# A two-layer graph network of 64 stages: one engine meeting at a stage's end for two, earlier parameter reads, row statistics inside two MLPs

## The reference

```python
xn = LN(x)
for l in range(2):                       # _L0_gnn: edge attention, 8 heads of 32
    q, k, v = h @ Wq, h @ Wk, h @ Wv     # h = xn at first
    a = exp(e - max_dst e);  e = sum(q[dst] * k[src]) / sqrt(32)
    h = LN(segment_sum(v[src] * a / z[dst]) @ Wo + h) * g + b
x = x + relu(h @ w1 + b1) @ w2 + b2  +  hyperbolic_mixer(xn)
y = LN(x)                                # _L0_ffn: an MLP on the top half of the rows by y @ wr
x = x + y + where(selected, (gelu(y @ w1 + b1) @ w2 + b2) * (y @ wr), 0)
xn = LN(x)
conv = segment_sum((xn @ W)[src] * norm) # _L1_gnn
y = xn
for l in range(4):                       # _L1_mix: linear-attention transformer
    q, k, v = softmaxes of LN(y) @ Wq, LN(y) @ Wk; LN(y) @ Wv
    y = y + (q @ (k.T @ v)) @ Wo + bo
    y = y + gelu(LN(y) @ W1 + b1) @ W2 + b2
x = x + conv + y
xn = LN(x)                               # _L1_ffn: graph attention (4 heads of 4) over 65,536 edges
scores = LN16(gat(xn @ W_gat)) meaned over heads;  top 2 of 4 experts, softmax weights
x = x + sum_e gate_e * (gelu(xn @ W1[e] + b1[e]) @ W2[e] + b2[e])
```

## Time and profile before

| | |
|---|---|
| time, median of 3 runs | 7004.79 us (7004.34 to 7008.51) |
| the profiled execution's own time | 6997.66 us |
| its span | 6995.9 us |
| PE, PEld busy | 5115.3, 3841.5 us (73%, 55%) |
| DVE busy | 4527.9 us (65%) |
| ACT busy | 2380.0 us (34%) |
| POOL busy | 4021.1 us (57%) |
| both edge-attention stages | 829.9 to 1984.7 and 2174.1 to 3325.4 us |
| rank MLP, its norm | 3410.4 to 3625.3, to 3645.3 us |
| token selection, routed MLP | to 3712.4, to 3915.6 us |
| norm, table pass, first transformer norm | to 3934.0, to 4007.4, to 4034.6 us |
| the transformer's four layers | to 5847.5 us, MLPs 235.5, 236.1, 235.5, 249.1 |
| experts | 5895.0 us to the end |

### The profile page before, as it was taken

One profiled execution on the slowest core, in us unless ns is written; L12 is line 12 of the kernel. 1 busy time (PEld: TensorE's weight loads), 2 busy tenths in 40 slices (PEclk: granted clock), 3 DMA queues, 4 the chain that ended last, 5 costly groups with the idle time before them and its releaser, 6 DMA issues. The chain is left out here.

```text
span 6995.9 us, 102505 instructions
## 1 busy us (share of the span) xinstructions
PE 5115.3 (73%) x27238; PEld 3841.5 (55%) x27238; DVE 4527.9 (65%) x7921; ACT 2380.0 (34%) x6607; POOL 4021.1 (57%) x4040
## 2 busy tenths in 40 slices
PE   3445588888857888887667579979889896877722
PEld 1334455555535555555556457768667575666611
DVE  8468499999966999998592375474654735211166
ACT  3143155555532555555212222222222221222210
POOL 1566577777737777775017656556555561577710
PEclk9777798999978999999888889989999997888855
DMA  2000377777725777775200223324333242222101
GB/s 43 24 1 5 113 224 220 219 219 218 219 62 160 224 222 220 218 217 158 54 14 7 66 72 104 110 68 115 88 92 112 64 125 67 46 45 59 25 2 59
DMA packets 362048, 766.30 MB, mean 110 GB/s; under 512 B 133276, under 2 KB 189493, under 8 KB 360552
## 3 DMA queue, kind: packets, MB, share of 16 engines
q0 software_dynamic: 232848, 605.63, 31.9%
q1 hardware_dynamic: 128707, 154.57, 7.3%
HBM read 717.16 MB, written 42.74 MB: 109 GB/s over the span
## 5 line engine op out<-in xcount | busy, mean ns | idle before, releaser
L1802 POOL DMA_INDIRECT arena<-kv_rows,visit_src x1616 | 1641.2, 1016 | 575.1 <-issue 467.6
L2378 POOL DMA_INDIRECT arena<-piece_rows,visit_src x808 | 798.6, 988 | 554.9 <-PE ps L2440 259.3
L2063 ACT CAST ps<-cat 125x265 bf16 x1616 | 619.6, 383 | 671.7 <-issue 385.5
L1955 PE MATMUL ps<-arena,w 125*128 x4848 | 787.3, 312 | 81.1 <-DVE stage_ht L1842 64.6
L924 POOL DMA_INDIRECT sorted<-arena,cat x512 | 541.1, 1057 | 514.4 <-PEq L91 338.5
L1955 PEld LDWEIGHTS ps<-arena,w 125*128 125x128 bf16 x4848 | 515.2, 106 | 373.6 <-issue 202.1
L2809 POOL DMA_INDIRECT arena<-tab,visit_src x537 | 512.6, 955 | 185.9 <-issue 172.3
L2064 ACT COPY arena<-ps x1616 | 604.6, 374 | 0.3
L924 POOL DMA_INDIRECT by_low<-steer x400 | 389.2, 973 | 373.3 <-PEq L91 162.3
L848 PE MATMUL ps<-stage_ht,w 128*128 128x250 f32 (+1 forms) x2496 | 555.9, 379 | 18.2 <-DVE stage_ht L880 13.1
L2459 DVE TENSOR_TENSOR arena<-arena,ps 125x256 f32 x808 | 340.1, 421 | 318.0 <-PE ps L2440 242.9
(11 more groups left out here) (605 smaller groups left out, 9697.0 us busy)
## 6 DMA issues: line engine op xcount, KB each, us to landing
w<-rel SPq DMA_DIRECT2D x102, 500.0 KB
arena<-kv_rows,visit_src POOLq DMA_INDIRECT x1616, 4.5
arena<-rel SPq DMA_DIRECT2D x34, 512.0 KB
arena<-piece_rows,visit_src POOLq DMA_INDIRECT x808
kv_rows<-h SPq DMA_DIRECT2D x50, 250.0 KB
arena<-tab,visit_src POOLq DMA_INDIRECT x537
sorted<-arena,cat POOLq DMA_INDIRECT x512
w<-in_L_mix_W SPq DMA_DIRECT2D x8, 1024.0 KB
```

The source lines that it names most:

```text
L1802: nc.gpsimd.indirect_dma_start(ring[k % RG][:, j, :], None, d.kv, bass.IndirectOffsetOnAxis(g.srcv[:, v:v + 1], 0)).then_inc(got[k % RG], 16)
L1955: ins = nc.tensor.matmul(psQ[:, j * D:(j + 1) * D], ohT[b % 4][:, e:e + EP], q[:, bass.ds(at[j], D)], start=(m == 0), stop=(m == 2))
L2063: nc.scalar.copy(flat[0:P, bass.ds(clean[j], WIDE)], zeros[:, 0:WIDE]).then_inc(s["zeroed"], 1)
L2378: nc.gpsimd.indirect_dma_start(self.rows[v % (self.RG * GG)], None, self.d.pieces, bass.IndirectOffsetOnAxis(g.srcv[:, v:v + 1], 0)).then_ ...
```

## The change

Five edits.

1. `phase`: the second meeting goes. In its place the numbers cleared by a stage "rest": they are allocated again at once under another name and released after the next stage's block, so that the next stage gets other numbers and the one after it may have them. As POOL's clears now go by runs of neighbouring numbers, the built program has 97 range clears for 76.
2. `graph_attention_layer`: the marks of POOL's scatters end three tiles earlier (second layer) and five earlier (first).
3. The norms of `routed_ffn` and `graph_convolution` issue no scatters and take no statistics. The rank MLP and the routed MLP take them, DVE one for each tile after its adds. The 24 scatters go to the routed MLP (162 for 150) and to the table pass (58 for 46).
4. The eight norms of the transformer's layers have no scatters. The first layer's first norm still has its gathers. Each QKV stage has 14 scatters for 10.
5. `experts`: the five rows of small parameters are fetched on SP's queue behind expert 0's weights, in the experts' norm, to places of their own; the two `loaded` waits become one wait for that fetch, in the table stage.

```diff
--- before.py
+++ after.py
@@ -35,8 +35,8 @@
-TABLE = 46
-INQKV, SOFT, INOUT, INMLP = 10, 16, 10, 23
+TABLE = 58
+INQKV, SOFT, INOUT, INMLP = 14, 16, 10, 23
@@ -90,8 +90,15 @@
     sems = [nc.alloc_semaphore(f"{n}_{COUNT[0]}") for n in names]
     with nc.Block() as block:
         yield block, dict(zip(names, sems))
+    for rested in RESTING:
+        nc.release_semaphore(rested)
+    RESTING.clear()
+    numbers = [sem.num for sem in sems]
     nc.clear_and_free_semaphores(sems)
-    nc.all_engine_barrier()
+    RESTING.extend(nc.alloc_semaphore(f"resting_{COUNT[0]}_{n}", num=n) for n in numbers)
+
+
+RESTING = []
@@ -1650,11 +1657,11 @@
             if not first:
                 g.proj_w.wait(pool)
                 nc.gpsimd.dma_start(d.h_kept, g.h).then_inc(s["side_b"], 16)
-                scatter.send_along(pool, left, EC - left, s["down"], range(1, NT + 1))
+                scatter.send_along(pool, left, EC - left, s["down"], range(1, NT - 2))
                 scatter.all_landed(pool)
                 pool.wait_ge(s["side_b"], 16)
             if first:
-                scatter.send_along(pool, left, EC - TAIL - left, s["down"], range(1, NT + 1))
+                scatter.send_along(pool, left, EC - TAIL - left, s["down"], range(1, NT - 4))
                 scatter.all_landed(pool, EC - TAIL)
@@ -2094,8 +2101,9 @@
 def routed_ffn(nc, g, a, d, scatter):
...
-    layernorm(nc, g, x, xn, side=together(scatter.beside(12), fetching(
-        (g.mlp_w, big_weights(g, a["L0_ffn_w1"], a["L0_ffn_w2"])), (g.small_b, small_weights(g, a["L0_ffn_b1"], a["L0_ffn_b2"])))))
+    layernorm(nc, g, x, xn, side=together(fetching(
+        (g.mlp_w, big_weights(g, a["L0_ffn_w1"], a["L0_ffn_w2"])), (g.small_b, small_weights(g, a["L0_ffn_b1"], a["L0_ffn_b2"])))),
+              counted=True)
@@ -2190,7 +2198,7 @@
     mlp(nc, g, xn, 1024, ACT.Gelu_apprx_tanh, x, g.coef[:, 0:NT], ready=[g.mlp_w, g.small_b],
-        side=together(scatter.along(150, "up", range(0, 4 * (NT + 1) // 2)), fetching((g.conv_w, [(w3(g.cat[:, 0:512], 2, D), split_k(a["L1_gnn_W"], 2))]),
+        stats=x, side=together(scatter.along(162, "up", range(0, 4 * (NT + 1) // 2)), fetching((g.conv_w, [(w3(g.cat[:, 0:512], 2, D), split_k(a["L1_gnn_W"], 2))]),
                                                     (g.proj_w, mixer_proj(g, a, 0)))))
@@ -2317,7 +2325,7 @@
 def graph_convolution(nc, g, a, d, scatter):
-    layernorm(nc, g, g.x, g.h, side=together(scatter.beside(12), before_layer(g, a, 0)))
+    layernorm(nc, g, g.x, g.h, side=before_layer(g, a, 0), counted=True)
     table_pass(nc, g, d, scatter)
     return Convolution(nc, g, d, scatter)
@@ -2465,8 +2473,7 @@
-    side = conv.beside(0, places=2, behind=2 if l else 0)
-    layernorm(nc, g, y, None, side=together(side, before_layer(g, a, l)) if l else side, counted=l > 0)
+    layernorm(nc, g, y, None, side=before_layer(g, a, l) if l else conv.beside(0), counted=l > 0)
@@ -2618,8 +2625,8 @@
     for l in range(4):
         linear_attention(nc, g, a, d, l, conv)
-        layernorm(nc, g, y, None, side=together(conv.beside(0, places=2, behind=2), fetching(
-            (g.small_b, small_weights(g, a["L1_mix_b1"][l], a["L1_mix_b2"][l]) + per_row(g, a["L1_mix_ln2_g"][l], a["L1_mix_ln2_b"][l])))),
+        layernorm(nc, g, y, None, side=fetching(
+            (g.small_b, small_weights(g, a["L1_mix_b1"][l], a["L1_mix_b2"][l]) + per_row(g, a["L1_mix_ln2_g"][l], a["L1_mix_ln2_b"][l]))),
                   counted=True)
         upcoming = (g.proj_w, mixer_proj(g, a, l + 1)) if l < 3 else (
             g.conv_w, [(w3(g.cat[:, 1536:1568], 2, 16), split_k(a["L1_ffn_W_gat"], 2))])
@@ -3108,7 +3115,11 @@
                  (one.brow, a["L1_ffn_b2"][e].rearrange("(a n) -> a n", a=1))]
         return fetching((one.here, big_weights(one, a["L1_ffn_W1"][e], a["L1_ffn_W2"][e]) + small))
-    layernorm(nc, g, x, xn, side=weights_of(0))
+    par = g.view(38816, 48, P)
+    aS, aD = g.view(38864, 16, P), g.view(38880, 16, P)
+    rows = [(par[:, 16 * n:16 * n + 16], a["L1_ffn_" + b].partition_broadcast(P)) for n, b in enumerate(("b_gat", "ln_gamma", "ln_beta"))]
+    rows += [(ap, a["L1_ffn_att_" + b].rearrange("h e -> (h e)").partition_broadcast(P)) for ap, b in ((aS, "src"), (aD, "dst"))]
+    layernorm(nc, g, x, xn, side=together(weights_of(0), fetching((g.small_a, rows))))
@@ -3129,14 +3140,11 @@
     tmp = g.view(13300, NT * 16, P)
-    aS, aD = g.view(13800, 16, P), g.view(13820, 16, P)
...
-    with phase(nc, g, "loaded", "step", "table", "ad", "spare", "stored", "ad_stored", "ad_back") as (block, s):
+    with phase(nc, g, "step", "table", "ad", "spare", "stored", "ad_stored", "ad_back") as (block, s):
         @block.sync
         def _(sp):
-            sp.dma_start(aS, a["L1_ffn_att_src"].rearrange("h e -> (h e)").partition_broadcast(P)).then_inc(s["loaded"], 16)
-            sp.dma_start(aD, a["L1_ffn_att_dst"].rearrange("h e -> (h e)").partition_broadcast(P)).then_inc(s["loaded"], 16)
             sp.wait_ge(s["spare"], 1)
             sp.dma_start(d.adt[N:WINDOWS * 128, :], spare[0:WINDOWS * 128 - N, :]).then_inc(s["ad_stored"], 16)
@@ -3153,7 +3161,7 @@
             V = nc.vector
             step = Steps(dve, s["step"])
             V.memset(spare, 0.0).then_inc(s["spare"], 1)
-            dve.wait_ge(s["loaded"], 32)
+            g.small_a.wait(dve)
@@ -3194,14 +3202,9 @@
-    par, scr, cmpb, rk4, ex, lower = take(48), take(100), take(400), take(100), take(100), take(16)
+    scr, cmpb, rk4, ex, lower = take(100), take(400), take(100), take(100), take(16)
...
-    with phase(nc, g, "loaded", "lowset", "step", "var", "std", "shifted", "expd") as (block, s):
-        @block.sync
-        def _(sp):
-            for n, b in enumerate((a["L1_ffn_b_gat"], a["L1_ffn_ln_gamma"], a["L1_ffn_ln_beta"])):
-                sp.dma_start(par[:, 16 * n:16 * n + 16], b.partition_broadcast(P)).then_inc(s["loaded"], 16)
-
+    with phase(nc, g, "lowset", "step", "var", "std", "shifted", "expd") as (block, s):
         @block.gpsimd
         def _(pool):
@@ -3229,7 +3232,6 @@
             step(V.tensor_tensor(s4, s4, rz.unsqueeze(2).to_broadcast([P, NT * H, EX]), ALU.mult))
-            dve.wait_ge(s["loaded"], 48)
             step(V.tensor_tensor(S3, S3, par[:, 0:16].unsqueeze(1).to_broadcast(w16), ALU.add))
@@ -3328,7 +3330,7 @@
             graph_attention_layer(nc, g, d, a["L0_gnn_Wo"][l], a["L0_gnn_ln_g"][l], a["L0_gnn_ln_b"][l], upcoming[l],
...
         rank = RankByHigh(nc, g, d, by_low)
-        mlp(nc, g, g.h, 1024, ACT.Relu, g.x, g.unit, ready=[g.mlp_w, g.small_b], weave=rank)
+        mlp(nc, g, g.h, 1024, ACT.Relu, g.x, g.unit, ready=[g.mlp_w, g.small_b], weave=rank, stats=g.x)
...
         by_dst = Scatter(nc, d.sorted, rank.places_i, rank.packed)
         routed_ffn(nc, g, a, d, by_dst)
```

## The result

The changed kernel took 6930.65 us (median of 4 runs, 6925.52 to 6933.11), the kernel before 7006.65 beside it (4 runs, 7004.34 to 7008.67): ratio 0.9898, 95% interval 0.9885 to 0.991. The forecast was 6934, the range 6912 to 6962. The two profiled spans are 6995.9 and 6928.6, 67.3 apart, the medians 76.0, for a sum of 70.7.

What follows compares the result with a forecast made beforehand. No one bound: each of 64 stages costs what its latest engine costs at the meeting. Terms -28 -11.1 -22.7 +9.3 -18.2 = -70.7 from the median 7004.8 give 6934 us, range 6912 to 6962.

Steps and rivals of the forecast that it cites:

- Second meeting, -28: At all 64 stage ends: removing the second meeting lets engines start earlier, less in POOL-led stages; -28 us, bounds -34 and 0.
- Marks, -7.8 and -3.3: Two attention projection stages: earlier scatter marks leave SP last in the first, -7.8 us; POOL paces the second, -3.3.
- Short norms, -22.7: Transformer norms without scatters: -15.1 before three layers, -6.6 before MLPs, -2.5 in the first, 1.5 charged for uncovered loads.
- Rank MLP, +4.5: Rank MLP: 25 added statistics lengthen DVE's late pairs; +4.5 us, bounds +1 and +12, the latter by PE's clock.
- Its norm, -9.2: Norm after the rank MLP: loses statistics, their loop and 12 scatters; -9.2 us.
- the convolution's, -8.6: Norm of the convolution: DVE loses 8.27 us and 0.3 of start; -8.6 us.
- Routed MLP, +10.0: Routed MLP, 162 scatters for 150: POOL already last, without pause in the steady part; 15.2 less 5.1 idle, +10.0 us.
- table pass, +12.6: Table pass, 58 scatters for 46: POOL already last, without pause; 15.2 less 2.6 idle, +12.6 us, bounds +5 and +15.
- Small parameters, -18.2: Earlier fetch ends DVE's waits: -2.6 us in the expert table stage, -15.6 for the gate stage, kept rows late next by 1.8.
- the code fetch: Rival: at each stage start a code fetch takes the meeting's place, first term about 0; 6962 us, chance 0.08.
- POOL's giving back: Rival: POOL ends four QKV stages later by 2 each, and both moved scatter lots cost their upper bound; 6950, chance 0.15.
- The fall of the clock: Rival: PE's granted clock falls in the edge-attention stages, some 90 us show; 7024 us, chance 0.02.

Runs made afterwards that it cites:

- the run with one meeting alone: The kernel before with only the second meeting removed and the cleared numbers resting, no other edit: 6974.8 us, ratio 0.9956.
- My later expectation of 6898: Expected for the changed kernel with scatters 144 in routed MLP, 40 in table pass, 13 per out projection, 29 per transformer MLP; measured 6905.9 us, ratio 0.9858.
- the whole spread with the levelled weave: Changed kernel with ranking rewoven in the rank MLP, scatters spread wider (136 in routed MLP, 40 in table pass), marks ended earlier there: 6870.1 us, ratio 0.9806.

## Why the prediction was right

By its own steps:

- **Second meeting, -28.** Put back 27.5 by spans, alone 28.6 by medians, 21 to 24 without the three stages that vary most. The size is right within what the runs tell; that two readings fall on 28 is in part luck. I charged POOL-led stages with 0.4 of 0.5; the runs don't resolve that part, as such stages vary by more than that.
- **Marks, -7.8 and -3.3.** -7.9 and -2.6, undone +7.5 and +1.9. Both signs and the new last engine are as said. The first size hits by luck: POOL stood 5.9 to 7.8 behind SP in the three kernels with all marks, and the stage varies by 4.5 with the same code. In the second stage POOL and SP meet within 0.1 us; its size, less than 1 us off, is not told apart from noise.
- **Short norms, -22.7.** The three before layers -15.8 without their meetings (15.1), the four before MLPs -7.2 (6.6), the first -2.4 (2.5); undone 26.0 in all, for 24.2. The 1.5 charged for what is uncovered was not there, and the QKV stages hide four more scatters, as costed.
- **Rank MLP, +4.5.** +5.3, undone 5.7, and 5.0 against the run with one meeting alone. This is a size that was off: I took off 1.5 for holes in DVE's late stream, and they went from 2.9 us (two pairs) to 2.1 only, which makes the term 5.2. The bound of +12 by the clock was not needed: PE's slow groups are there in both traces (8.5 to 9.8 us after idle gaps of 2 to 4 us, 7.04 else), and DVE sets the pace meanwhile. By the Trainium skill's "TensorE: Matmul & The Clock Gate", section HAM oscillation, the term would have been nearer +10; the groups agree with it, the stage's length doesn't, since there was slack in PE.
- **Its norm, -9.2; the convolution's, -8.6.** -9.0 and -9.3. In the first the statistics alone are 7.9, 1.3 under the term, and the meeting has the rest; in the second -8.8 against the run with one meeting alone.
- **Routed MLP, +10.0; table pass, +12.6.** +10.0 and +11.0, POOL last in both. But the terms were for the scatters, and taking 12 out of each gave 11.5 and 11.4: the first is 1.5 over its term and the second 1.2 under, and the routed MLP's +10.0 is 11.5 less the 1.5 that one meeting alone took off that stage. So its hit is luck. The reading behind the first term was wrong: before, POOL did not idle 8.6 us in the first pairs, but 3.7, and 5.4 in six waits for marks later on. The step "no pause in the steady part" holds at 162, not at 150. In both stages 12 scatters closed some 5 us of idle time and lengthened POOL's end behind the last scatter by 1.0, for which the sum had nothing. My later expectation of 6898 missed by the same step.
- **Small parameters, -18.2.** -2.9 and -15.3 without three meetings, and +2.8, +18.3, -2.0 when undone. The kept rows were late next, as the price assumed: a wait of 2.58 and not 1.8.

Of the rivals, the code fetch falls with the two runs on the meeting, and by "Runtime: NRT & Kernel Launch", section Instruction fetch mechanics, of the Trainium skill a gap would have had to appear behind the release, where ACT's work still starts 0.1 behind it. The two pauses in the norm behind the rank MLP, 0.7 us longer in all without the meeting, are the one sign for it. POOL's giving back falls with the QKV stages. The fall of the clock didn't come, as the windows of both edge-attention stages show (the first for the last line of the earlier trace rows):

```profile
821.50:1972.50 1151.00, 930.39 (x4605) 627.05 (x4605) 1040.45 (x1579) 634.08 (x2074) 821.70 (x808) 0.90 0.73 211
2156.80:3307.20 1150.40, 931.61 (x4605) 628.78 (x4605) 1040.11 (x1579) 635.50 (x2075) 826.13 (x808) 0.90 0.73 211
```

The granted clock is 0.90 in both. The first is 3.5 us shorter than before, which is within what it varies by.

That the sum was near is also the work of opposite errors: the scatters in the routed MLP are 1.5 over their term and the rank MLP 0.8, the scatters in the table pass are 1.2 under, and the 1.5 charged for uncovered loads didn't come. Which engine ends each edited stage was right in every term.

## What to carry to other kernels

When all engines meet after each stage, price an edit by the distance between the last and the second last engine at that meeting, and read both from the drains; that held here for the marks and the short norms. An engine that is last in a stage costs its own pace for each instruction given to it, less what it idled (15.2 us of scatters cost 11.5), and nothing in a stage where it is done early, so small background work belongs to the stages with room: moving 24 scatters gave 23 us of stage time, and the whole spread with the levelled weave 60 us. Background work that is spread over progress marks must have its last mark earlier than the stage's end by the time of its last pieces and of the tail behind them, or fewer pieces gain next to nothing.

## What the runs showed of the hardware

POOL's drain at a meeting is long behind scatters: 10.6, 13.4 and 15.6 us behind 136, 150 and 162 in the routed MLP, 17.0 behind 58 in the table pass, 3.3 behind two in a norm and 7.4 behind two beside 2 MB of loads, 52 ns with none. It isn't all waiting for data. The drain's record begins while POOL still issues; in the changed kernel's routed MLP it begins at 3886.8, and this is the last scatter:

```profile
3897.27 0.96 POOL L931 DMA_INDIRECT sorted<-arena,cat  x1 [0.31 <-issue]
```

It ends at 3898.2, and POOL arrives at 3902.4. So of 15.6 us 11.4 are scatters and 4.2 come behind the last one. That tail is 3.2 behind 150 in the run with the scatters moved to the transformer's MLPs, 2.4 behind 136 (where the drain is 10.6 or 6.8, by where the marks end) and 4.9 behind the 58 of the table pass. A scatter given to POOL costs its 0.96 and 0.30 on the engine, and the tail is 1.0 longer for twelve more of them in both stages. The release of an engine that waits at a meeting costs little: in about half of the changed kernel's stages the first work starts 0.08 to 0.13 us behind it and in most others 0.3 to 0.4, with the clears of POOL beside it.
